# Two transformer layers on one core: the end of the first attention in another order

## The chip, the core and the metric

One core of a Trainium2 chip runs the whole program. Its engines are TensorE (PE, with its weight loads PEld), VectorE (DVE), ScalarE (ACT), GpSimd (POOL) and SyncE (SP), which only issues DMAs here. The metric is the device time of one launch in microseconds.

## The reference

Four residual steps on x of shape (2, 1024, 128), each on a layernorm of x. The change lies between the end of the first and the beginning of the routed part of the second.

```
x = x + attention0(layernorm(x))   # 8 heads, low-rank queries and keys, softmax over 1024 keys, W_O
x = x + ffn0(layernorm(x)):
      shared = (silu(h @ shared_gate.T) * (h @ shared_up.T)) @ shared_down.T       # width 352
      probs = softmax(h @ gate_w.T); the 2 best of 8 experts, weights normed
      routed = sum over the 2 experts of weight * the same ffn with the expert's weights
x = x + attention1(layernorm(x))   # 16 heads of 8, rope, causal
x = x + ffn1(layernorm(x))         # 2 of 8 experts for the whole sequence, gelu
```

## The kernel before

The 2048 tokens are 16 tiles of 128, 4 chunks of 512, 2 batches of 1024. There is no planner: each engine has its own list of instructions, in an order written out by hand, and the lists meet in semaphores (`wait_ge`, `then_inc`). An engine that waits holds up all that stands behind it in its list.

**The first attention** runs in 16 units (u = 0 to 15) of two heads. In a unit, k goes over 8 key tiles of 128. For each k there are four `scores` (i = 0 to 3: two heads by two query chunks), ACT's exponentials of them (`exp0`, L907), and `values` (L1353), which multiplies them by the compressed values. The denominators are sums of the exponentials over the keys: the tiles of a pair of k are added (`pair_adds` on POOL, `last_sums` on DVE in the last unit, L2079), and `denominators(u, pp, j)` (L1361) multiplies the sum of pair j by ones, for j = 0 to 3. `exp0` for an even k waits until the pair sum before it has read the same buffer. `denominators` of j = 0 waits for `rden_ok`, the four reciprocals (`context_rden`, L2070) of the unit before, which read the same PSUM bank; the unit's own last one (j = 3) is called in the next unit. In the table `DEN0_AT` stands at which k which j is called.

In the last unit PE has no scores for maxima to do, and other work lies beside it: the norm of batch 0 is turned (`second_turns`), `gate_logits(0, c)` are made at k = 2 and 3, DVE makes `probabilities(0)`, `probabilities_normed(0)`, `ranks(0)` and, after PE's `expert_counts(0)` (at k = 7), `slots(0)`, which gives the row that each token goes to.

**From the last unit to the routed blocks.** POOL's `scatter(0)` is 16 indirect DMAs (L641) that wait for `slot_ok`. SP's `load(0)` (L510) waits for all of them, and PE's `block_x_turns(0)` (L1597) for the load. ACT and DVE split the turned rows into a high and a low part (`block_x_hi`, `block_x_lo`), and `block_up(0)` (L1624 to L1626) is the first product of the routed experts. It also waits for the low parts of all eight experts' weights (`w_lo_ok`) and for the table of experts (`block_ok`). Four experts' weights are split early; for the `LATE_EXPERTS` ACT makes `hi_weights` and DVE `low_weights` (L2203).

Meanwhile the rest of the attention and the shared expert run: the last `denominators`, `last_context` (four reciprocals and two products, L2088), `o_mms(2)` and `o_mms(3)` (output products of batch 1, L1374), `add_output1` (L2096), `second_stats`, `half_var`, `quick_rstd` (the norm's factor), `norm_chunk(2)` and `norm_chunk(3)` (L1967), `second_turns(2)` and `(3)` (L1387), `gate_logits(1, ...)` (L1393). The shared expert goes by chunk c and third f of its width: `shared_up(c, f)` (L1540, gate and up), ACT's `shared_silu` (L1018), DVE's `shared_hidden(c, f)` (L2334), then `shared_down(c)` (L1554) and `shared_add(c)` (L2339). In the kernel before only chunks 0 and 1 are done here. `shared_up` number n = 3c + f waits for `h_done` n - 1, n = 1 for the context's bank and n = 3 for the bank of the denominators.

Of the kernel before, what the change touches and what calls it, by code (L numbers as in the profile page):

```python
# [46 lines left out]
NCH = T // CH  # L47
# [86 lines left out]
Z0_FIRST = 2  # L134
Z0_AT = {1: (1, 3), 3: (2, 0), 4: (2, 1)}
TURN0_AT = {(5, 1): 0, (6, 0): 1, (6, 1): 2, (7, 0): 3}
DEN0_AT = {3: 0, 5: 1, 7: 2}

# [84 lines left out]
def build(nc, d, out):  # L225
    with ExitStack() as ctx:
# [206 lines left out]
            g = HP * ((c + pp) % 2) + h  # L433
            return slice(DC * g, DC * (g + 1))
        XT_BANK, ROUTE_BANKS, XNT1_BANKS, OUT_BANKS = 7, (7, 6), (0, 1, 6, 7), (2, 2, 4, 5)
        DOWN_BANKS = (4, 5, 6, 3)
        FRONT_BANKS = (6, 6, TURN1_BANK, TURN1_BANK)

        OUT1_TURN_BANKS, OUT1_BANKS, LAST_BANKS = (0, 1, 4, 5), (0, 1, 6, 7), (0, 1, 4, 5)
# [417 lines left out]
        def _(act):  # L857
# [152 lines left out]
            def shared_silu(c, fs=range(3)):  # L1010
                for f in fs:
                    n, m = 3 * c + f, FM[f]
                    act.wait_ge(eg_mm, n + 1)
                    if n == 0:
                        act.wait_ge(pair_add, U0 * NPAIR * HQ)
                    if n >= 2:
                        act.wait_ge(h_done, n - 1)
                    nc.scalar.activation(silu_pt(n)[0:m], ps[0:m, gate_bank(n), :], ACT.Silu).then_inc(silu_done, 1)  # L1018

            shared_silu(0, range(2))  # L1020
            for e in LATE_EXPERTS:
                hi_weights(e)
            shared_silu(0, range(2, 3))
            shared_silu(1)
            second_xnT(2)
            second_xnT(3)
# [223 lines left out]
        def _(pe):  # L1250
# [126 lines left out]
            def second_turns(c):  # L1377
                pe.wait_ge(ln_xn, NT + (c + 1) * TC)
                if c == 0:
                    pe.wait_ge(max_done, U0 * NMX0)  # L1380
                if c == 2:
                    pe.wait_ge(ctx_T, U0)
                    pe.wait_ge(h_done, 2)
                if c == 3:
                    pe.wait_ge(slot_ok, 1)
                for t in range(TC):
                    ins = nc.tensor.transpose(ps[:, XNT1_BANKS[c], t * P:(t + 1) * P], xn[:, c * TC + t, :], ident[:])  # L1387
                ins.then_inc(ln_turn, 1)
# [22 lines left out]
            def unit0(u, pp):  # L1411
# [10 lines left out]
                for k in range(TS):  # L1422
# [10 lines left out]
                        values(u - 1, 1 - pp, TS - 1)  # L1433
                    if k == 1 and u:
                        denominators(u - 1, 1 - pp, NPAIR - 1)
                    if k in DEN0_AT:
                        denominators(u, pp, DEN0_AT[k])
                    turn(k, 0)
                    for i in range(2, HQ):
                        scores(u, pp, k, i)  # L1440
# [101 lines left out]

            def shared_down(c, ts=range(TC)):
                pe.wait_ge(h_done, 3 * c + 3)
                if c < 2:
                    pe.wait_ge(o_add, 3 + c)
                elif c == 2:
                    pe.wait_ge(slot_ok, B)
                else:
                    pe.wait_ge(h_done, 3 * c + 2)  # L1550
                for t in ts:
                    for f in range(3):
                        m = FM[f]
                        ins = mm(ps[:, DOWN_BANKS[c], t * P:(t + 1) * P], hidden_pt(3 * c + f)[0:m, t * P:(t + 1) * P],  # L1554
                                 wm[0:m, E0, 2 * F0 + f * D:2 * F0 + (f + 1) * D], start=(f == 0), stop=(f == 2))
                if TC - 1 in ts:
                    ins.then_inc(ed_mm, 1)

            pe.wait_ge(wm_in, 16)
            denominators(U0 - 1, 1, NPAIR - 1)  # L1560
            shared_up(0, range(2))
            for c in range(2, NCH):
                o_mms(c)
            shared_up(0, range(2, 3))
            shared_up(1)
            shared_down(0)
            second_turns(2)
            second_turns(3)
            shared_down(1)
            gate_logits(1, 0)  # L1570
# [391 lines left out]
        def _(dve):  # L1962
# [118 lines left out]
            def last_context(u):  # L2081
                for q in range(4):
                    context_rden(u, q)
                dve.wait_ge(rden_ok, 4 * (u + 1))
                dve.wait_ge(ctx_T, u + 1)
                for c in range(QH):
                    rows = half_rows(u, c)
                    v.tensor_tensor(ctxT[rows, u // UH, u % UH // 2, c, :], cT[rows, 1, :], cT[rows, 0, :],  # L2088
                                    ALU.mult).then_inc(ctx_out, 1)
# [256 lines left out]
            ranks(0, 1)  # L2346
            slots(0)
            last_sums(3)
            block_experts(0)
            last_context(U0 - 1)  # L2350
            shared_hidden(0, 0)
            shared_hidden(0, 1)
            for n, e in enumerate(LATE_EXPERTS):
                dve.wait_ge(w_hi_ok, n + 1)
                low_weights(e)
            for c in range(2, NCH):
                add_output1(c)
                second_stats(c * TC, (c + 1) * TC)
                shared_hidden(0 if c == 2 else 1, 2 if c == 2 else 0)
            half_var(1, 1)  # L2360
            quick_estimate(1)
            shared_hidden(1, 1)
            quick_newton(1)
            shared_hidden(1, 2)
            quick_newton(1)
            quick_newton(1)
            dve.wait_ge(half_step, hs.n)
            norm_chunk(2)
            norm_chunk(3)
            shared_add(0)  # L2370
            shared_add(1)
            probabilities(1)

# [379 lines left out]
```

## Time and profile before

| what | value |
|---|---|
| median of 3 runs | 847.03 us (844.85, 847.03, 851.38) |
| profiled execution | 852.06 us, its span 850.2 us |
| mean granted clock of TensorE | 0.974 of full |
| PE busy | 778.2 us, 92% |
| DVE, ACT, POOL busy | 613.6, 505.9, 411.1 us |

Times in all rows are microseconds from the span's start of the one profiled execution. A value in brackets at the end of a row is how long the engine was idle before it, and the instruction that ended this idle time. The granted clock is in parts of full speed: 1.00 is 2.4 GHz and 0.50 is 1.2 GHz.

### The profile page before, as it was taken

The page shows a single profiled execution, that of the slowest core. Times are in us where ns is not written, and L with a number is a line of the kernel's source. Part 1 is how long each engine was busy: PE and PEld are TensorE (multiplying, and loading weights), DVE is VectorE, ACT ScalarE, POOL GpSimd, SP SyncE. Part 2 cuts the span into 40 slices and gives each one's busy share as a digit, 9 for nine tenths or more (in the row PEclk, how much of TensorE's full clock was granted, in tenths as well). Part 3 has the DMA queues.
Part 4 walks back from the last instruction along what each step waited for, and adds up shares of the span by engine and source line. Part 5 has one row for each costly group of instructions (what it writes and reads, how often), then busy time and mean ns, then how long its engine had stood idle before and what let it go on. Part 6 is the DMA issues. An engine that isn't in the chain of part 4 may idle for free.

```text
span 850.2 us, 13859 instructions
## 1 busy us (share of the span) xinstructions
PE 778.2 (92%) x4602; PEld 454.9 (54%) x4602; DVE 613.6 (72%) x1611; ACT 505.9 (59%) x864; POOL 411.1 (48%) x466
## 2 busy tenths in 40 slices
PE   5899999999999988889999988789999999999986
PEld 2354444444444433378978865445555455554554
DVE  5878687786877895966336669777778778788555
ACT  3336665757656574445646555467767777776672
POOL 3505866677666682634242577886353232220121
PEclk9979999999999996999999999899999999999999
DMA  9300000000000000022222112000000000000001
GB/s 348 147 18 1 1 1 1 1 1 1 1 1 1 2 1 1 31 85 82 66 81 70 35 37 83 22 10 1 1 2 1 1 2 1 1 1 1 2 1 50
DMA packets 14539, 25.35 MB, mean 30 GB/s; under 512 B 3174, under 2 KB 9192, under 8 KB 14344
## 3 DMA queue, kind: packets, MB, share of 16 engines
q1 hardware_dynamic: 11798, 18.85, 6.5%
q0 software_dynamic: 2048, 4.20, 1.7%
q10 hardware_dynamic: 626, 1.43, 0.5%
q8 instruction: 40, 0.66, 0.3%
q14 instruction: 27, 0.22, 0.1%
HBM read 15.03 MB, written 9.44 MB: 29 GB/s over the span
## 4 chain that ended last, share of the span: by engine, by line
PE 36%; DVE 15%; POOL 6%; issue 3%; ACT 1%; DMA 0%; ACTq 0%; POOLq 0%; DVEq 0%
PE ps L1671 6%; PE ps L1756 6%; PE ps L1736 4%; DVE ps L2529 3%; PE ps L1642 3%; DVE mx_part L2532 3%; PE ps L1624 2%; PE ps L1626 2%; PE ps L1625 2%; PE ps L1634 1%; POOL xnT L659 1%; PE ps L1540 1%; PE ps L1589 1%; PE ps L1764 1%; PE ps L1825 1%
## 5 line engine op out<-in xcount | busy, mean ns | idle before, releaser
L2047 DVE TENSOR_REDUCE mx_part<-ps 128x1 f32<-128x512 f32 x256 | 163.8, 682 | 58.5 <-PE ps L1320 57.8
L1112 ACT ACTIVATE pt<-ps 128x1024 f32<-128x1024 f32 (+1 forms) x160 | 149.7, 938 | 69.5 <-PE ps L1736 68.2
L907 ACT ACTIVATE pt<-ps 128x512 f32<-128x512 f32 x256 | 140.9, 596 | 76.8 <-PE ps L1345 70.0
L1671 PE MATMUL ps<-rounded 128*128 128x128 f32 (+2 forms) x352 | 124.3, 387 | 11.5 <-DVE mx_part L2529 3.8
L2529 DVE CUSTOM_DVE_ANT_0 ps<-ps,wm 128x128 f32<-128x128 f32 (+3 forms) x256 | 119.5, 518 | 18.3 <-PE ps L1671 17.1
L1345 PE MATMUL ps<-rounded 100*128 100x512 f32 x256 | 122.3, 491 | 10.3 <-ACT pt L907 9.5
L859 ACT ACTIVATE rounded<-ps 128x512 fp32r<-128x512 f32 (+3 forms) x160 | 94.4, 592 | 62.3 <-PE ps L1309 22.1
L722 POOL TENSOR_SCALAR_AFFINE_SELECT pt<-pt 128x512 f32<-128x512 f32 x64 | 39.9, 636 | 167.1 <-ACT pt L1112 167.0
L1736 PE MATMUL ps<-rounded 128*128 128x512 f32 (+2 forms) x352 | 115.5, 368 | 0.7 <-ACT rounded L859 0.7
L1320 PE MATMUL ps<-rounded 98*128 98x512 f32 x256 | 104.9, 427 | 2.6 <-DVE mx_part L2047 1.4
L2532 DVE TENSOR_REDUCE mx_part<-ps 128x1 f32<-128x512 f32 x128 | 82.4, 686 | 30.9 <-PE ps L1671 30.5
L1345 PEld LDWEIGHTS ps<-rounded 100*128 100x128 f32 x256 | 47.6, 192 | 83.2 <-ACT pt L907 46.7
L1671 PEld LDWEIGHTS ps<-rounded 128*128 128x128 f32 x352 | 64.1, 192 | 45.8 <-DVE mx_part L2532 19.5
L1756 PE MATMUL ps<-pt,wm 128*9 128x512 f32 (+3 forms) x768 | 77.8, 493 | 5.5 <-POOL pt L722 5.4
L1736 PEld LDWEIGHTS ps<-rounded 128*128 128x128 f32 x352 | 62.5, 188 | 37.4 <-issue 17.8
L588 POOL TENSOR_TENSOR xn<-pt 128x512 f32<-128x512 f32 x48 | 60.3, 1280 | 46.0 <-ACT pt L907 46.0
L588 POOL TENSOR_TENSOR xnT<-pt 128x512 f32<-128x512 f32 x48 | 60.4, 1279 | 33.3 <-ACT pt L907 33.3
L1353 PE MATMUL ps<-pt,ckv 128*32 128x512 f32 x512 | 69.9, 619 | 0.9 <-ACT pt L907 0.9
L1320 PEld LDWEIGHTS ps<-rounded 98*128 98x128 f32 x256 | 48.8, 193 | 25.8 <-issue 19.4
L641 POOL DMA_INDIRECT to_experts<-xn,slot_i x32 | 33.9, 1060 | 45.8 <-DVE slot_i L2297 36.6
L2469 DVE TENSOR_TENSOR pt<-ps,pt 128x352 f32<-128x352 f32 x46 | 24.1, 523 | 40.5 <-ACT pt L1059 39.8
L859 ACT ACTIVATE pt<-ps 128x128 f32<-128x128 f32 (+2 forms) x94 | 36.4, 388 | 22.4 <-PE ps L1634 13.6
(308 smaller groups left out, 1296.4 us busy)
## 6 DMA issues: line engine op xcount, KB each, us to landing
wm<-in_wm SPq DMA_DIRECT2D x1, 4896.0 KB, 15.8
to_experts<-kstage SPq DMA_DIRECT2D x6, 512.0 KB, 4.6
of_experts<-pt SPq DMA_DIRECT2D x12, 256.0 KB, 2.0
kstage<-to_experts SPq DMA_DIRECT2D x10, 256.0 KB, 2.8
wm<-in_experts SPq DMA_DIRECT2D x1, 1540.0 KB, 7.6
x<-in_x SPq DMA_DIRECT2D x4, 256.0 KB, 6.2
out<-x SPq DMA_DIRECT2D x4, 256.0 KB, 2.3
early<-in_wo ACTq DMA_DIRECT2D x1, 512.0 KB
```

The source lines that it names most:

```text
L588: nc.gpsimd.tensor_tensor(sums(u, j)[i], pt0(0, i), pt0(1, i), ALU.add).then_inc(pair_add, 1)
L859: return nc.scalar.activation(dst, src, ACT.Copy)
L907: nc.scalar.activation(pt0(k, i), ps[:, ST0_BANKS[i % 2], :], ACT.Exp, scale=SCALE0).then_inc(exp_done, 1)
L1112: nc.scalar.activation(pt[:, 4 * (t % 2) + 2 * g:4 * (t % 2) + 2 * g + 2, 0:w], ps[:, ST1_BANKS[2 * g]:ST1_BANKS[2 * g] + 2, 0:w], ACT.Exp ...
L1320: mm(ps[:, max_bank(u, n), :], cq[0:NZ, b * S + j * P:b * S + (j + 1) * P], key_stack[u % 2][0:NZ, h, c * CH:(c + 1) * CH], start=True, st ...
L1345: mm(ps[:, ST0_BANKS[i % 2], :], key_stack[pp][0:NZM, h, k * P:(k + 1) * P], query_stack[pp][0:NZM, h, c * CH:(c + 1) * CH], start=True, s ...
L1671: ins = mm(bank[:, o:o + w], queries1(u, i), keys[:, 0:w], start=(o == 0), stop=(o == parts[-1][1]))
L1736: ins = mm(ps[:, ST1_BANKS[r], o:o + w], keys[:, j % TC * P:(j % TC + 1) * P], queries1(u, (c + 1) * TC - w // P, w // P), start=(o == 0), ...
L1756: ins = mm(ps[RS * r:RS * r + DH + 1, CTX_BANK, CH - w:CH], v_cur[pp][:, j, r, :], pt[:, 4 * (t % 2) + r, o:o + w], start=(j == CTX1_START ...
L2047: v.tensor_reduce(mx_part[u % 2][:, o:o + 1], ps[:, max_bank(u, n), :], AX_X, ALU.max).then_inc(max_done, 1)
L2529: v.tensor_tensor_reduce(tile, tile, later[:, CH - w:CH], 1.0, NEG, ALU.add, ALU.max, dst).then_inc(max1_done, 1)
L2532: v.tensor_reduce(dst, tile, AX_X, ALU.max).then_inc(max1_done, 1)
```

## The change

It computes the same and has the same instructions. In the last unit `denominators` of pair 0 is called at k = 4 instead of k = 3. On PE `shared_up(0, 0)` goes ahead of the unit's last `denominators`, the other two thirds of chunk 0 ahead of `o_mms`, `shared_down(0)` ahead of `shared_up(1)`, and the last third of `shared_up(1)` between `second_turns(2)` and `second_turns(3)`. `shared_down(0)` writes bank 7 instead of 4 and waits for `slot_ok` instead of `o_add`; `second_turns(3)`, which writes bank 7 as well, waits for `shared_add(0)`. On DVE `shared_hidden(0, 0)` goes between the first and the second reciprocal, the other two of chunk 0 behind the context products, the norm's factor is computed in one piece, `shared_add(0)` goes ahead of the norm, and `low_weights` and `block_experts(0)` go behind it. On ACT the third silu goes between the second and the third `hi_weights`.

```diff
-DEN0_AT = {3: 0, 5: 1, 7: 2}
+DEN0_AT, DEN0_LAST_AT = {3: 0, 5: 1, 7: 2}, {4: 0, 5: 1, 7: 2}
...
-        DOWN_BANKS = (4, 5, 6, 3)
+        DOWN_BANKS = (7, 5, 6, 3)
...
             shared_silu(0, range(2))
-            for e in LATE_EXPERTS:
+            for e in LATE_EXPERTS[:2]:
                 hi_weights(e)
             shared_silu(0, range(2, 3))
+            for e in LATE_EXPERTS[2:]:
+                hi_weights(e)
             shared_silu(1)
...
                 if c == 3:
-                    pe.wait_ge(slot_ok, 1)
+                    pe.wait_ge(moe_add, 1)
...
-                    if k in DEN0_AT:
-                        denominators(u, pp, DEN0_AT[k])
+                    den_at = DEN0_AT if u + 1 < U0 else DEN0_LAST_AT
+                    if k in den_at:
+                        denominators(u, pp, den_at[k])
...
             def shared_down(c, ts=range(TC)):
                 pe.wait_ge(h_done, 3 * c + 3)
-                if c < 2:
-                    pe.wait_ge(o_add, 3 + c)
+                if c == 0:
+                    pe.wait_ge(slot_ok, 1)
+                elif c == 1:
+                    pe.wait_ge(o_add, 4)
...
             pe.wait_ge(wm_in, 16)
+            shared_up(0, [0])
             denominators(U0 - 1, 1, NPAIR - 1)
-            shared_up(0, range(2))
+            shared_up(0, range(1, 3))
             for c in range(2, NCH):
                 o_mms(c)
-            shared_up(0, range(2, 3))
-            shared_up(1)
             shared_down(0)
+            shared_up(1, range(2))
             second_turns(2)
+            shared_up(1, [2])
             second_turns(3)
             shared_down(1)
...
             def last_context(u):
                 for q in range(4):
                     context_rden(u, q)
+                    if q == 0:
+                        shared_hidden(0, 0)
...
             last_sums(3)
-            block_experts(0)
             last_context(U0 - 1)
-            shared_hidden(0, 0)
             shared_hidden(0, 1)
+            shared_hidden(0, 2)
+            for c in range(2, NCH):
+                add_output1(c)
+                second_stats(c * TC, (c + 1) * TC)
+            half_var(1, 1)
+            quick_rstd(1)
+            shared_add(0)
+            norm_chunk(2)
+            shared_hidden(1, 0)
+            norm_chunk(3)
+            shared_hidden(1, 1)
             for n, e in enumerate(LATE_EXPERTS):
                 dve.wait_ge(w_hi_ok, n + 1)
                 low_weights(e)
-            for c in range(2, NCH):
-                add_output1(c)
-                second_stats(c * TC, (c + 1) * TC)
-                shared_hidden(0 if c == 2 else 1, 2 if c == 2 else 0)
-            half_var(1, 1)
-            quick_estimate(1)
-            shared_hidden(1, 1)
-            quick_newton(1)
-            shared_hidden(1, 2)
-            quick_newton(1)
-            quick_newton(1)
-            dve.wait_ge(half_step, hs.n)
-            norm_chunk(2)
-            norm_chunk(3)
-            shared_add(0)
+                if n == 0:
+                    shared_hidden(1, 2)
+            block_experts(0)
             shared_add(1)
             probabilities(1)
```

## Rows read from the trace of the kernel before

**Rows 1.** The page: the granted clock in 40 slices of 21.3 us.
```profile
PEclk9979999999999996999999999899999999999999
```

**Rows 2.** Windows: busy time of each engine, granted clock (PEclk), DMA.
```profile
320.50:321.00 0.50, 0.00 (x0) 0.00 (x0) 0.50 (x1) 0.00 (x0) 0.50 (x1) 0.77 0.00 0
...
334.00:334.50 0.50, 0.50 (x8) 0.00 (x0) 0.50 (x2) 0.00 (x0) 0.00 (x0) 0.58 0.00 0
...
344.00:348.00 4.00, 2.35 (x17) 0.54 (x18) 3.76 (x9) 1.83 (x3) 2.61 (x3) 1.00 0.05 16
...
375.50:376.00 0.50, 0.50 (x3) 0.50 (x3) 0.23 (x2) 0.48 (x2) 0.00 (x0) 0.50 0.59 225
```

**Rows 3.** Timeline of PE in the last unit: start, duration, instruction, count.
```profile
319.15 1.06 PE L1353 MATMUL ps<-pt,ckv 128*32 128x512 f32 x8
321.33 1.94 PE L1361 MATMUL ps<-half,ones 128*32 128x512 f32 x8 [1.11 <-DVE cT L2070]
...
341.25 1.04 PE L1361 MATMUL ps<-half,ones 128*32 128x512 f32 x8
```

**Rows 4.** Timeline of ACT in the last unit.
```profile
324.03 1.08 ACT L907 ACTIVATE pt<-ps 128x512 f32<-128x512 f32 x2 [3.89 <-PE ps L1345]
...
335.30 2.27 ACT L907 ACTIVATE pt<-ps 128x512 f32<-128x512 f32 x4 [3.12 <-PE ps L1345]
```

**Rows 5.** Timeline of DVE in the last unit.
```profile
317.90 3.38 DVE L2070 RECIPROCAL cT<-ps 128x128 f32<-128x128 f32 x4
...
324.66 1.29 DVE L2079 TENSOR_TENSOR early<-pt 128x512 f32<-128x512 f32 x2 [2.24 <-ACT pt L907]
...
330.87 0.22 DVE L2226 TENSOR_REDUCE g<-g 128x8 f32<-128x64 f32 x1 [4.36 <-ACT g L935]
...
333.67 1.29 DVE L2079 TENSOR_TENSOR half<-pt 128x512 f32<-128x512 f32 x2
...
340.48 0.22 DVE L2267 TENSOR_TENSOR big<-ps,kcount 128x64 f32<-128x64 f32 x1 [1.71 <-PE ps L1407]
...
343.98 2.50 DVE L2079 TENSOR_TENSOR early<-pt 128x512 f32<-128x512 f32 x4
```

**Rows 6.** Timeline of PE from the last unit to the first block.
```profile
346.62 1.06 PE L1361 MATMUL ps<-early,ones 128*32 128x512 f32 x8 [1.66 <-DVE early L2079]
347.62 3.70 PE L1540 MATMUL ps<-xnT,wm 128*128 128x512 f32 x8
351.92 3.84 PE L1374 MATMUL ps<-vo,big 128*128 128x128 f32 x32 [0.60 <-DVE big L2088]
...
368.48 2.84 PE L1554 MATMUL ps<-wm,pt 128*128 128x128 f32 x24
...
372.86 0.64 PE L1597 MATMUL ps<-ident,kstage 128*128 128x128 f32 x4
375.01 0.42 PE L1624 MATMUL ps<-rounded 128*128 x1 [1.51 <-DVE x_lo L2463]
```

**Rows 7.** Timeline of DVE after the last unit.
```profile
353.70 3.28 DVE L2203 TENSOR_TENSOR rounded<-wm,rounded 128x704 fp32r<-128x704 f32 x4
356.90 0.68 DVE L2096 TENSOR_TENSOR x<-ps,x 128x512 f32<-128x512 f32 x1
...
363.81 0.69 DVE L2334 TENSOR_TENSOR pt<-ps,pt 96x512 f32<-96x512 f32 x1 [0.43 <-PE ps L1540]
...
365.66 2.27 DVE L1967 TENSOR_SCALAR xn<-x,mv,lnv 128x128 f32<-128x128 f32 x8
```

**Rows 8.** Timeline of POOL: the eighth and the last of sixteen scatters.
```profile
354.26 3.55 POOL L641 DMA_INDIRECT to_experts<-xn,slot_i  x1 [0.30 <-issue]
...
366.95 0.95 POOL L641 DMA_INDIRECT to_experts<-xn,slot_i  x1 [0.30 <-issue]
```

**Rows 9.** SyncE's DMA queue: two first loads; landing of the first five.
```profile
369.19 0.80 SPq L510 DMA_DIRECT2D kstage<-to_experts  x2
...
DMA to landing us min/median/max: 2.7/3.0/3.7
```

## The prediction

> **What bounds the kernel now.** I read the page first: TensorE (PE) is busy 92% of the span (the table above), and the row of granted clock has one dent inside the first attention's end, at the slice that begins near 319 us [rows 1]. Then the windows: the clock falls between 320.5 and 321 us from 2.4 to 1.2 GHz and comes back at 334.1, while a stretch with more idle PE, 344 to 348, keeps it [rows 2]. Then the timelines of PE, ScalarE (ACT) and VectorE (DVE) over the last unit, and of PE, DVE, GpSimd (POOL) and SyncE's queue from there to the first routed block. The reader should see two stages. Up to 344 us a loop over the three engines is in charge, not PE's load: the exponentials of key tile k+1 need the pair sums of DVE, these need the exponentials of tile k, these PE's scores. From 344 to 375 us a chain that alternates between PE and DVE is in charge, with POOL's sixteen scatters as a second chain close beside it. From 375 us on PE is nearly full, so what is won before it should reach the end whole: nothing later is tied to an absolute time.
>
> **Part 1, denominators(15, 0) from k = 3 to k = 4.** In front of PE's scores (3,2) and (3,3) stands denominators of pair 0, which waits for the reciprocals of unit 14. DVE makes these from 317.90 to 321.28; PE stands 1.11 us and starts at 321.33, by then at 1.2 GHz [rows 3, 5]. Behind it come the scores, their exponentials at 324.03 after 3.89 us of idle ACT, their sums at 324.66 after 2.24 us of idle DVE [rows 3 to 5].
> After the change scores (3,2) follow values(2) at about 320.1 (319.15 and 1.06 us [rows 3]; their bank is free by then). Their exponentials (2.27 us for four, 0.57 each) lie under the reciprocals. DVE goes on without a gap: four sums at 0.62 us from 321.2 end at 323.7 and probabilities(0), which needs gate_logits(0,1) at 321.3, at 324.2. The eight gate logits are 0.8 us (sixteen fit in between 371.3 and 372.86 [rows 6]). PE at 2.4 GHz does scores (4,0) and (4,1), values(3) (1.0) and denominators(0) (1.0, as the row at 341.25) from 321.3 and reaches scores (4,2) at 323.6; exponentials (4,2) and (4,3) end at 325.1, the gate's at 325.35. So probabilities_normed starts at 325.4, where it was 330.87: 5.5 us earlier. From there the steps of before: 2.8 us to last_sums(2) (330.87 to 333.67), four sums 2.5 (ends 330.7), the rest of the ranks about 1.5 (before, DVE's last piece ended at 338.77, that is 340.48 less the wait of 1.71), expert_counts about 0.5 (an estimate below that wait of 1.71), so slots(0) begins at 332.7 instead of 340.48, **7.8 us** earlier; before, the exponentials (5,2) to (6,1) only came at 335.30 because denominators(1) and values(4) ran at half clock [rows 3 to 5]. The last exponential is done at 336.0 and slots at 336.2, so last_sums(3) (343.98 before) moves by the same 7.8.
> How much of this is order and how much clock? The same hand schedule for the old order at 2.4 GHz throughout: denominators(0) 321.33 to 322.25, exponentials (3,2) and (3,3) to 323.7, sums to 324.4, exponentials of tile 4 to 326.5, normed at 326.8, slots at 334.1. So the order is worth **1.4 us** and the clock's fall **6.4 us**. The fall is one event of one execution.
>
> **Part 2, from last_sums(3) to the first block.** I keep the times of before (last_sums(3) at 343.98) and take off the shift at the end. One third of shared_up is four matmul instructions, 1.72 us (3.44 between first and last start of eight, plus the tail). shared_up(0,0) fits in PE's wait of 1.66 us ahead of the last denominators, which stay at 346.62 [rows 6]. DVE then has nothing in 346.4 to 347.7 (block_experts, 1.3 us, stood there for free and now costs DVE 1.3 us later). Reciprocal 0 (0.85, a quarter of 3.38 [rows 5]) to 348.6, shared_hidden(0,0) 0.6 (like the one at 363.81 [rows 7]), three reciprocals and the context product: first half at 352.5, 0.6 us later than before. PE does shared_up(0,1) and (0,2) to 351.1 and waits 1.3 us; output products 352.5 to 356.05 (3.56 between starts, against 351.92), shared_down(0) 2.7 us to 358.75, no longer behind add_output1; shared_up(1,0..1) to 362.2.
> DVE: two hidden products to 354.3, first add and statistics to 356.2, second add at 356.35. From 356.90 to 365.66 before are 8.8 us, of which four hidden products (0.6 each) and the wait of 0.43 fall away and 1.8 are the first chunk: 4.1 us, so the norm is known at 360.5 [rows 7]. shared_add(0) to 361.2; norm_chunk(2) to 362.35, hidden(1,0) to 362.95, norm_chunk(3) to 364.1, hidden(1,1) to 364.7, first low part (0.82 us of the 3.28) to 365.5, hidden(1,2) to 366.15. PE: turns of chunk 2 at 362.4, shared_up(1,2) 363.0 to 364.8, turns of chunk 3, wait of 0.8 for hidden(1,2), shared_down(1) 366.2 to 368.9 (368.48 to 371.16 before), gate logits 1.7 us: block_x_turns(0) could start at **370.6** instead of 372.86. Three low parts and block_experts end at 369.9, ahead of block_up(0), which costs nothing while its cover, the 2.15 us from block_x_turns(0) to block_up(0), stays. The moved wait of second_turns(3) for moe_add 1 (shared_add(0), 361.2) is over before norm_chunk(3); the split of the high weights on ACT lies in ACT's idle time.
> The other chain is POOL's. Its last scatter ends at 367.9, the load is issued at 369.19 and took 2.7 to 3.7 us (its line in rows 9), so the rows were there between 371.9 and 372.86: without a faster scatter the gain is at most 1.0 us. One scatter took 3.55 us, the others 0.96 [rows 8, 9]. It began at 354.26, inside DVE's four low parts (353.70 to 356.98) and ended 0.83 after them. I take it that these products with both inputs in SBUF hold up POOL. The change puts the low parts at the end of the scatters: 2.6 us less, and perhaps 1.0 again on the sixteenth. Load landed between 369.3 and 371.3. Value taken: 371.0, a gain of **2.0 us** (bounds 0 and 2.3).
> The Trainium skill, "SBUF — State Buffer", section "Who interferes with whom", infers that a tensor_tensor leaves descriptor generation alone; by that, the long scatter has another cause and stays, and this term is at most 1.0 instead of 2.0. The row speaks against the page, as a coincidence in time only.
>
> **The sum.** Against the profiled execution (852.06 us, span 850.2): 7.8 + 2.0 = 9.8, hence 842.3. Against the median of 847.03: the three runs lie at 844.85, 847.03 and 851.38, and 852.06 less the fall's 6.4 is 845.7, so I read the lower two as runs without it and the upper one as one with it. Then the median loses 1.4 + 2.0 = 3.4: 843.6. Between the two, I predict **843.0**.
>
> **Rivals.**
> (a) The fall is in most executions of before and the change always removes it: 847.03 - 9.8 = 837.2. For it: the profiled run and one of three show it, and the change removes just the wait in which it fell. Against: the middle run lies nearer to the lowest than to the highest. 0.16.
> (b) The clock falls at another wait, slower than before. The price is the 6.4 us just worked out, the place PE's new wait of 1.3 us ahead of the output products or the one at expert_counts (about 0.7, after scores with gaps); 843.0 + 6.4 = 849.4. It decides if the fall comes in more than half of the executions. For it: 1.11 us of idle was enough at 320.2, and 1.51 ahead of 375.01, where the clock is down at 375.5. Against: 1.66 us at 345 was not, and PE's waits from 344 to 375 add up to about 3.8 us instead of 5.3 [rows 2, 6]. 0.18.
> The Trainium skill, "TensorE: Matmul & The Clock Gate", section "A second HAM failure mode: psum-queue depth-cycling", says that frequent short idles between groups of matmuls make the clock oscillate; by that rule this rival would be the outcome, and the trace agrees in one of the two waits that are longer than 1.5 us.
> (c) The scatter stays long, or the late low parts and block_experts hold up the first block: part 2 gives 0 to 1.0, so 844.0 to 845.0. 0.18.
> (d) My forecast, 840 to 845: 0.48.
>
> **Range and chances.** Clear of no change by this kernel's measurement is about 1%, 8.5 us. The range takes in (c), (d) and half of each of (a) and (b): 837.5 to 848.5. Faster by over 1% (under 838.6) is (a), 0.16, and 0.01 for the dip at 375 gone as well: 0.17. Slower by over 1% (over 855.5) would need two falls: 0.04. The rest, 0.79, is within 1%.
>
> **What would show it.** Right: no PE wait for cT ahead of L1361 near 321; ACT's idle of 3.89 us and DVE's of 4.36 much shorter; slots at least 1.4 us earlier; no scatter over 3 us in the middle of the sixteen; time from last_sums(3) to block_up(0) 29.0 us where it was 31.0; the granted clock full from 316 to 370. Wrong: PEclk at 0.50 anywhere from 322 to 370, DVE's second add later than 12.4 us after last_sums(3), SyncE's first load still 25.4 us after slot_i, or PE waiting for L2203 or L2311 ahead of L1624.

## The result and the profile after

The changed kernel takes 841.66 us (median of 20 runs, 838.84 to 847.80) where the kernel before, run beside it, takes 847.24 (20 runs, 842.09 to 854.46): ratio 0.9946, 95% interval 0.9926 to 0.9966. That is 5.6 us or 0.5% faster, inside the 1% that I had named as this kernel's bound, and 1.3 us from the 843.0 predicted. Here and below a ratio leaves disturbed runs out on both sides, so it can differ a little from the quotient of the medians beside it. On another chip, as the experiments show, the same kernel is 1.1% slower than the one before.

The profiled execution took 842.36 us, its span is 840.5 where it was 850.2. The page's row of the clock has no dent near 319 us any more (compare [rows 1]):

```profile
PEclk9879999999999999999999999999999999999999
```

The windows of the changed kernel confirm it; columns as in [rows 2]. From 316 to the first block the granted clock is 1.00, and it stays so when the block begins, where it was 0.50 before:

```profile
316.00:364.50 48.50, 42.33 (x258) 22.68 (x257) 40.94 (x108) 22.60 (x40) 24.03 (x21) 1.00 0.14 46
364.50:366.00 1.50, 1.48 (x8) 1.23 (x9) 0.65 (x3) 1.47 (x3) 0.00 (x0) 1.00 0.66 175
```

The timeline of PE, beside [rows 3] and [rows 6]:

```profile
321.25 1.04 PE L1363 MATMUL ps<-half,ones 128*32 128x512 f32 x8
...
336.32 1.98 PE L1543 MATMUL ps<-xnT,wm 128*128 128x512 f32 x4
338.24 1.06 PE L1363 MATMUL ps<-early,ones 128*32 128x512 f32 x8
...
344.13 3.84 PE L1376 MATMUL ps<-vo,big 128*128 128x128 f32 x32 [1.20 <-DVE big L2096]
...
357.88 2.94 PE L1559 MATMUL ps<-wm,pt 128*128 128x128 f32 x24 [0.62 <-DVE pt L2342]
360.67 1.85 PE L1395 MATMUL ps<-gw,xnT 128*128 128x8 f32 x16
362.37 0.63 PE L1603 MATMUL ps<-ident,kstage 128*128 128x128 f32 x4
364.52 0.42 PE L1630 MATMUL ps<-rounded 128*128 x1 [1.51 <-DVE x_lo L2468]
```

The reader should see that the denominators at 321.25 have no wait in brackets (1.11 us before), that shared_up(0, 0) at 336.32 fills the wait that stood ahead of the last denominators, and that block_x_turns(0) at 362.37 follows the gate logits with no wait: its rows had landed, PE's own order sets its start. DVE, beside [rows 5] and [rows 7]:

```profile
316.02 3.38 DVE L2076 RECIPROCAL cT<-ps 128x128 f32<-128x128 f32 x4
319.32 2.42 DVE L2085 TENSOR_TENSOR early<-pt 128x512 f32<-128x512 f32 x4
...
324.02 0.22 DVE L2234 TENSOR_REDUCE g<-g 128x8 f32<-128x64 f32 x1 [1.89 <-ACT g L935]
...
331.90 0.23 DVE L2275 TENSOR_TENSOR big<-ps,kcount 128x64 f32<-128x64 f32 x1 [1.02 <-PE ps L1409]
...
335.40 2.50 DVE L2085 TENSOR_TENSOR early<-pt 128x512 f32<-128x512 f32 x4
...
348.02 0.68 DVE L2104 TENSOR_TENSOR x<-ps,x 128x512 f32<-128x512 f32 x1
...
356.35 0.88 DVE L2211 TENSOR_TENSOR rounded<-wm,rounded 128x704 fp32r<-128x704 f32 x1
...
357.75 2.48 DVE L2211 TENSOR_TENSOR rounded<-wm,rounded 128x704 fp32r<-128x704 f32 x3
```

POOL and SyncE's queue, beside [rows 8] and [rows 9]. No scatter is longer than the first one, and the load is issued 2.3 us after the last begins:

```profile
336.21 1.59 POOL L641 DMA_INDIRECT to_experts<-xn,slot_i  x1 [11.66 <-DVE slot_i L2305]
...
356.20 0.95 POOL L641 DMA_INDIRECT to_experts<-xn,slot_i  x1 [0.30 <-issue]
```
```profile
358.45 0.80 SPq L510 DMA_DIRECT2D kstage<-to_experts  x2
```

**Where the 9.7 us between the two profiles lie.** I use two stages in all that follows. Stage 1 runs from the first of unit 14's four reciprocals to last_sums(3); stage 2 from there to block_up(0). Stage 1 was 317.90 to 343.98, 26.08 us, and is 316.02 to 335.40, 19.38. Stage 2 was 31.03 and is 29.12. So 6.70 and 1.91 us are the change's; another 1.88 had arisen before it (317.90 against 316.02), where nothing was changed, and 0.79 was given back behind block_up(0) (475.19 against 475.98 us to the end of the span). The sum is 9.70.

### The profile page after: what moved, and what is told of

It reads as the page before. It is cut to its first block, busy times and chain, and to the rows that moved or that the text cites. A ratio compares the mean times of both kernels' runs of the same rounds, so it can differ in the third digit from the quotient of the medians.

```text
span 840.5 us, 13859 instructions
## 1 busy us (share of the span) xinstructions
PE 770.1 (92%) x4602; PEld 451.0 (54%) x4602; DVE 613.3 (73%) x1611; ACT 505.5 (60%) x864; POOL 408.9 (49%) x466
## 4 chain that ended last, share of the span: by engine, by line
PE 36%; DVE 14%; POOL 6%; issue 4%; ACT 2%; DMA 0%; ACTq 0%; POOLq 0%; DVEq 0%
PE ps L1677 6%; PE ps L1762 6%; PE ps L1742 4%; DVE ps L2534 3%; PE ps L1648 3%; DVE mx_part L2537 3%; PE ps L1630 2%; PE ps L1640 2%; PE ps L1631 2%; PE ps L1632 2%; POOL xnT L659 1%; PE ps L1595 1%; PE ps L1770 1%; PE ps L1831 1%; PE ps L1543 1%
## 5 line engine op out<-in xcount | busy, mean ns | idle before, releaser
L1355 PE MATMUL ps<-pt,ckv 128*32 128x512 f32 x512 | 68.2, 605 | 0.9 <-ACT pt L907 0.9
L641 POOL DMA_INDIRECT to_experts<-xn,slot_i x32 | 31.8, 992 | 41.5 <-DVE slot_i L2305 32.4
L859 ACT ACTIVATE pt<-ps 128x128 f32<-128x128 f32 (+2 forms) x94 | 36.3, 388 | 22.6 <-PE ps L1640 13.8
```

The source lines that it names most:

```text
L859: return nc.scalar.activation(dst, src, ACT.Copy)
```

## The experiments

Theory: stage 1 gains 1.4 us by order and the rest by the clock; stage 2 gains since DVE's low parts no longer hold up a scatter. Rivals: the clock falls anyway at another wait; the long scatter has another cause. Four kernels ran on each of three chips, called S, T and U, with the kernel before beside them. A stage is read from the one profiled execution of each kernel. Its median was 878.47 on S, 877.34 on T and 846.52 on U.

| kernel | chip | median us | ratio to before (95%) | stage 1 | stage 2 | longest scatter after the first |
|---|---|---|---|---|---|---|
| a_den_only | S | 876.65 | 0.9963 (0.9928 to 0.9997) | 19.38 | 31.05 | 3.56 |
| b_rest_only | S | 889.97 | 1.0143 (1.0082 to 1.0204) | 20.70 | 41.5 | 1.18 |
| c_low_early | S | 878.81 | 1.0003 (0.9972 to 1.0033) | 19.39 | 33.21 | 4.10 |
| d_low_late | S | 889.67 | 1.0118 (1.0068 to 1.0168) | 20.70 | 43.2 | 0.96 |
| after_again | T | 888.07 | 1.0108 (1.0049 to 1.0167) | 19.40 | 41.5 | 1.19 |
| e_den_low | T | 887.79 | 1.0106 (1.0053 to 1.0159) | 19.39 | 43.2 | 0.96 |
| f_fill | T | 878.51 | 1.0008 (0.9981 to 1.0036) | 20.68 | 31.08 | 3.56 |
| g_turn_early | T | 888.36 | 1.0119 (1.0070 to 1.0168) | 19.39 | 41.65 | 1.21 |
| before_again | U | 846.40, one run | | 20.70 | 31.08 | 3.55 |
| h_one_pause | U | 843.96 | 0.9988 (0.9958 to 1.0017) | 19.38 | 31.75 | 2.70 |
| i_three_pauses | U | 844.27 | 0.9997 (0.9971 to 1.0024) | 19.38 | 32.35 | 2.69 |
| j_early_three | U | 844.71 | 0.9980 (0.9951 to 1.0010) | 19.39 | 33.09 | 2.70 |

**a_den_only**, the kernel before with the new place of the denominators alone.
```diff
-DEN0_AT = {3: 0, 5: 1, 7: 2}
+DEN0_AT, DEN0_LAST_AT = {3: 0, 5: 1, 7: 2}, {4: 0, 5: 1, 7: 2}
...
-                    if k in DEN0_AT:
-                        denominators(u, pp, DEN0_AT[k])
+                    den_at = DEN0_AT if u + 1 < U0 else DEN0_LAST_AT
+                    if k in den_at:
+                        denominators(u, pp, den_at[k])
```


> The kernel before with one edit: in the last unit denominators of pair 0 is called at k = 4. Stage 1 is the time from the first reciprocal of unit 14 to last_sums(3) (26.1 us before, 19.4 after the change), stage 2 from last_sums(3) to block_up(0) (31.0 before, 29.1 after). Order theory: stage 1 is 19.4 us if the clock stays at 2.4 GHz, stage 2 stays at 31.0; median 1.4 us under before, and up to 3 us if falls of the clock near the reciprocals become rarer. Rival, clock only: the order itself gives nothing, stage 1 of a run of the old order without a fall is also 19.4, and the median differs from before by less than 1 us unless the falls vanish.

**b_rest_only**, the changed kernel without it.
```diff
-DEN0_AT, DEN0_LAST_AT = {3: 0, 5: 1, 7: 2}, {4: 0, 5: 1, 7: 2}
+DEN0_AT, DEN0_LAST_AT = {3: 0, 5: 1, 7: 2}, {3: 0, 5: 1, 7: 2}
```


> The changed kernel with denominators of pair 0 back at k = 3. Stage 2 is 29.1 us as in the changed kernel, the sixteen scatters have none over 1.6 us. Stage 1: with a fall of the clock 26 us, without one 20.8 (order theory) or 19.4 (clock only). Median: before less 1.9 us.

Stage 1 is 19.38 against 20.70 us: with the clock full in both, the order alone is worth 1.3. In a the rest is as before, long scatter and stage 2 of 31.05 included, and its median gains 1.8 us. But b is 1.4% slower, which no theory of mine had: stage 2 takes 41.5 us. Its chain of waits, in order of time, names what:

```profile
349.45 0.28 DVE mv L2112 x4
349.73 9.48 another core or an unknown queue
359.21 0.02 issue
359.24 0.70 DVE x L2104
```

Only one core runs, so the 9.48 us between the first chunk's statistics and the second chunk's addition are a wait that the profile can't name.

**c_low_early**, the changed kernel with the low parts ahead of the two output additions, so that they lie in the middle of the scatters again.
```diff
             shared_hidden(0, 2)
+            for n, e in enumerate(LATE_EXPERTS):
+                dve.wait_ge(w_hi_ok, n + 1)
+                low_weights(e)
             for c in range(2, NCH):
...
             shared_hidden(1, 1)
-            for n, e in enumerate(LATE_EXPERTS):
-                dve.wait_ge(w_hi_ok, n + 1)
-                low_weights(e)
-                if n == 0:
-                    shared_hidden(1, 2)
+            shared_hidden(1, 2)
```


> The changed kernel with the four low parts of the weights back ahead of the output additions. Port theory: one scatter that begins beside them takes about 3.5 us, as before; the norm is known 3.3 us later and block_x_turns(0) comes 2.5 to 3.3 us later than in the changed kernel, stage 2 about 32. Rival (what the Trainium skill, SBUF - State Buffer, section Who interferes with whom, infers for tensor_tensor): all scatters stay near 0.96 us, and the long one of before had another cause; stage 2 is then the same 32, as PE and DVE set it.

**d_low_late**, the kernel before with nothing but the same loop moved the other way, behind norm_chunk(3).
```diff
-            for n, e in enumerate(LATE_EXPERTS):
-                dve.wait_ge(w_hi_ok, n + 1)
-                low_weights(e)
             for c in range(2, NCH):
...
             norm_chunk(3)
+            for n, e in enumerate(LATE_EXPERTS):
+                dve.wait_ge(w_hi_ok, n + 1)
+                low_weights(e)
             shared_add(0)
```


> The kernel before with one edit: the four low parts go behind norm_chunk(3). Port theory: no scatter over 1.6 us in the middle, the first load is issued about 2.6 us earlier counted from slot_i (25.4 before). The chain of DVE loses 3.3 us ahead of the norm, PE's own work then sets the end: stage 2 about 29.3, nearly all of what the whole change wins in stage 2. Rival, the orders on PE and of the denominators carry it: stage 2 stays within 0.7 us of 31.0.

The long scatter follows the low parts. Timelines of DVE and POOL of c_low_early:

```profile
343.27 3.28 DVE L2211 TENSOR_TENSOR rounded<-wm,rounded 128x704 fp32r<-128x704 f32 x4
```
```profile
341.78 1.21 POOL L641 DMA_INDIRECT to_experts<-xn,slot_i  x1 [0.30 <-issue]
343.29 4.10 POOL L641 DMA_INDIRECT to_experts<-xn,slot_i  x1 [0.30 <-issue]
347.69 0.95 POOL L641 DMA_INDIRECT to_experts<-xn,slot_i  x1 [0.31 <-issue]
```

The scatter ends at 347.39, 0.84 us after the last low part (346.55). Before, the same two ends were 357.81 and 356.98, 0.83 apart; in a_den_only and f_fill they are 0.84 apart. In d_low_late all fifteen later ones take 0.96 or less. So the cause is the low parts, and the price is set by where they end. The 1.21 us in the changed kernel fits too: that scatter began at 344.42, beside the last context product (64x512, both inputs in SBUF), which ended at 344.79, and ended 0.84 us after it. But not every such instruction holds a scatter to its end: the four sums of `last_sums(3)` (128x512, inputs in SBUF, 335.40 to 337.90) lie beside the first scatter, which took 1.59 us, and it was done at 337.80, before the last sum.

c also divides what stage 2 gained. It does not stall in batch 0, and its stage 2 of 33.21 us, where I had expected about 32, stands against 29.12 in the changed kernel: in the new order the place of the low parts is worth 4.1 us. The rest of the new order without it is 2.2 us worse than the old one (33.21 against 31.05 in a_den_only). Together they make the 1.9 us. This compares profiles of different chips; where nothing stalls, the old order's stage 2 is the same on all of them (31.03, 31.05, 31.08 and 31.08).

The stall came back in d, with 43.2 us in stage 2, and not in c. So it is not part of the new order of PE or of the denominators: moving the low parts behind the scatters is enough to bring it.

**after_again** is the changed kernel itself, **e_den_low** the kernel before with the edits of a and d together.

> The changed kernel itself, as the measure for the other three on the same chip. Stage 1 (first reciprocal of unit 14 to last_sums(3)) 19.4 us, stage 2 (last_sums(3) to block_up(0)) 29.1, the ratio to before 0.995.

> The kernel before with two edits: denominators of pair 0 at k = 4, the four low parts behind norm_chunk(3). Nothing else of the change. If the place of the low parts carries stage 2: stage 1 19.4, stage 2 29.3 (PE's own work sets it), all scatters under 1.6 us, median within 1 us of the changed kernel. Rival, the new orders on PE and of the denominators carry it: stage 2 above 30.3 and the median 1.5 to 2 us above the changed kernel.

Both stall and are 1.1% slower than the kernel before on chip T. The windows of after_again, over the scatters of batch 0 and then of batch 1:

```profile
346.00:356.00 10.00, 4.54 (x28) 3.78 (x28) 1.84 (x9) 0.00 (x0) 7.83 (x9) 0.86 0.14 49
392.00:400.00 8.00, 4.62 (x32) 3.91 (x30) 5.94 (x24) 2.32 (x5) 6.13 (x7) 1.00 0.30 109
400.00:412.00 12.00, 3.66 (x15) 3.39 (x15) 0.53 (x1) 1.23 (x3) 9.25 (x10) 0.68 0.16 54
```

The columns are PE, PE's loads, DVE, ACT, POOL, the clock, the DMA share, GB/s. While POOL goes on at its pace of one in 1.27 us, PE is busy for a third to a half of the time and DVE and ACT hardly at all. The waits that the trace names no cause for ("remote" or "issue") give the times. The timelines of DVE and ACT:

```profile
357.88 0.69 DVE L2104 TENSOR_TENSOR x<-ps,x 128x512 f32<-128x512 f32 x1 [9.51 <-remote]
```
```profile
400.67 0.28 ACT L859 ACTIVATE pt<-ps 128x128 f32<-128x128 f32 x1 [4.58 <-remote]
```
```profile
407.18 0.53 DVE L2474 TENSOR_TENSOR pt<-ps,pt 128x352 f32<-128x352 f32 x1 [8.66 <-remote]
```

The row of batch 0 lasts from 334.56 to 355.37, and DVE stands from 348.37, 13.8 us after it began. The row of batch 1 lasts from 392.04 to 412.03; ACT stands from 396.09, 4.1 us after it began, and DVE from 398.52. So the stall doesn't begin at a fixed place in the row. It ends with the row: by 3 us after it all three engines run again.

The kernel before on chip U, in the corresponding stretches of its batch 1, has DVE, ACT and PE at work (scatters from 381.67 to 401.67):

```profile
381.00:389.00 8.00, 7.71 (x55) 6.90 (x55) 7.00 (x29) 4.76 (x11) 5.80 (x6) 1.00 0.33 107
389.00:401.00 12.00, 11.80 (x92) 11.51 (x91) 3.99 (x8) 7.50 (x18) 8.95 (x11) 1.00 0.38 118
```

And a_den_only, on chip S, has the stall in batch 1's scatters and in the gathers, where nothing interrupts the row, but not in batch 0's, where the eighth scatter took 3.56 us:

```profile
346.00:356.00 10.00, 9.42 (x39) 5.00 (x39) 9.82 (x33) 2.71 (x6) 8.26 (x6) 1.00 0.13 42
383.00:391.00 8.00, 5.00 (x35) 4.27 (x33) 6.29 (x26) 2.48 (x6) 5.81 (x6) 1.00 0.35 107
391.00:403.00 12.00, 3.91 (x15) 3.47 (x15) 0.53 (x1) 0.74 (x2) 9.20 (x10) 0.54 0.17 56
```

This divides the eight kernels on S and T without exception: a, c and f, whose scatter of batch 0 is interrupted in the middle by the low parts, don't stall there; b, d, e, g and the changed kernel do. Whether it is the interruption that keeps the stall away, or only that the low parts lie inside the row and not behind it, these kernels can't tell, since in them the two always go together. The kernel before is some 30 us slower on these chips than on U. Its other rows of indirect DMAs, which nothing interrupts, would account for much of it if they stall as a's do (DVE's waits with no cause named are 12.07 us in batch 1's scatters, 7.17 and 6.55 us in the gathers), but it was not profiled there.

**f_fill**, the kernel before with one product that nobody reads ahead of the wait for the reciprocals, to fill part of it.
```diff
+                    if u == U0 - 1 and k == 3:
+                        pe.wait_ge(wm_in, 16)
+                        mm(ps[:, 0, :], wm[:, E0, 0:P], wm[:, 0, 0:CH], start=True, stop=True)
                     if k in DEN0_AT:
```


> The kernel before with one matmul of 128x512 on data that nobody reads (two instructions, 0.86 us) put into PE's wait of 1.11 us ahead of denominators of pair 0. Its order is the old one. If the clock falls because PE stands there, the falls near that place vanish and the median drops by their share times 5.4 us (0.5 to 2.5 us), with a higher mean granted clock than before, and stage 1 is 20.7 us. Rival, the fall has nothing to do with that wait: mean granted clock and median as before, within 1 us.

Stage 1 is 20.68 us and the ratio 1.0008, so the fill gains nothing that can be measured on T: at most 1.7 us by the interval's end. If the clock fell at this wait in most executions there, the median should have moved by most of 5.4.

**g_turn_early**, the changed kernel with block_x_turns(0) in the middle of shared_down(1) and the gate logits ahead of both, the DVE and ACT orders to match.
```diff
-            shared_down(1)
             gate_logits(1, 0)
             gate_logits(1, 1)
+            shared_down(1, range(0, 2))
...
             block_x_turns(0)
+            shared_down(1, range(2, TC))
```


> The changed kernel with a new end of stage 2: gate_logits(1) ahead of shared_down(1), so that the exponentials of the gate and both table loads of ACT lie under PE's work; block_x_turns(0) between the two halves of shared_down(1), so that the split of the rows lies under the second half. Expected: block_up(0) 1.2 us earlier (stage 2 27.9) and the first block's silu about 2 us earlier, so 2.0 us under the changed kernel. Rival: the load of the rows lands too late for the earlier turns, or the wait moves to DVE's low parts, and the median stays within 0.7 us of the changed kernel.

The wait ahead of block_up(0) fell from 1.51 to 0.17 us, but the stall of batch 0's scatters (stage 2 of 41.65) hid what that is worth. It was tried again in j.

The last four were meant for a chip that stalls; the one they ran on, U, behaves like that of the first profiles. **before_again** is the kernel before. **h_one_pause** is the changed kernel with an existing memset of 1.8 us on POOL moved into the middle of scatter(0); **i_three_pauses** has such a memset in scatter(0), in scatter(1) and between the two gathers; **j_early_three** is i with g's order.
```diff
+            def pause(n):
+                if n:
+                    pool.wait_ge(first_zero, n)
+                nc.gpsimd.memset(first_stack[:, 0:HG, :].bitcast(F32), 0.0).then_inc(first_zero, 1)
...
                 for k in range(TOPK):
+                    if k:
+                        pause(b)
                     for i in range(TS):
...
             scatter(0)
-            nc.gpsimd.memset(first_stack[:, 0:HG, :].bitcast(F32), 0.0).then_inc(first_zero, 1)
             scatter(1)
...
             gather(0)
+            pause(2)
             gather(1)
...
-                    dve.wait_ge(first_zero, 1)
+                    dve.wait_ge(first_zero, 3)
```


> The kernel before, unchanged, to have its own trace from the chip on which the other kernels of this study ran and took some 30 us more than on the first one. If the long stalls belong to uninterrupted trains of sixteen indirect DMAs on this chip: PE and DVE stand in the second half of scatter(1) and of the gathers, but not in scatter(0), whose 8th DMA is stretched to about 3.55 us by the low parts; span about 875 us. If they belong to something that the change brought: no stall of more than 3 us in the trains here, and the 30 us lie spread over the whole kernel. It also says whether the clock falls at the wait for the first four reciprocals here as in the first profile (then first reciprocal to last_sums(3) is about 26 us, otherwise 20.7).

> The changed kernel, with GpSimd's memset of first_stack (1.8 us, which stood behind scatter(0)) put between the 8th and the 9th indirect DMA of scatter(0). Theory (on this chip a train that runs on past some eight indirect DMAs makes the other engines stand, and the 2.6 us for which the low parts held up the 8th one in the kernel before kept that away): the stall of some 11 us in scatter(0) goes, last_sums(3) to block_up(0) is 30 to 32 us where the changed kernel had 41.5 here, and the time is about 877 where it was 888. Rival (low parts placed behind the train are the cause, by themselves, and no pause helps; or the number of DMAs in all counts): block_up(0) stays at 41 us or more from last_sums(3) and the time at 888.

> The changed kernel, with the same memset of 1.8 us three times: in the middle of scatter(0), in the middle of scatter(1), and between gather(0) and gather(1); the reader of first_stack waits for the third. Theory (pauses break the trains): no stall of more than 3 us on PE or DVE in any train, about 11 us less in scatter(0) and together some 25 us less in scatter(1) and the gathers, so some 850 us on this chip, 3% below the kernel before. Rival (only scatter(0) gains, since the stalls of scatter(1) and the gathers have another cause): 877. Rival (no pause helps): 888 to 892.

> The kernel of three pauses, with the block's turns of x ahead of the last three of unit 1's shared products, and its low parts ahead of the second shared addition (the order of g_turn_early). In g_turn_early PE waited only 0.17 us ahead of the first routed product where the changed kernel waits 1.51, but the stall of scatter(0) hid what that is worth. If that wait bounds: 1 to 2 us below the kernel of three pauses, about 849. If what PE gains there is lost behind (the scatter's landing bounds the first block, not the order of PE's work): the same as it within 0.5 us. If pauses do nothing: 888.

Whether a pause keeps the stall away could not be read, as chip U doesn't stall in any of them. What U did show are three other things.

First, the clock. before_again has the very wait in which it fell in the first profile, 1.11 us ahead of the same instruction, and it did not fall. The timeline of PE and the window around it:

```profile
318.01 1.06 PE L1361 MATMUL ps<-half,ones 128*32 128x512 f32 x8 [1.11 <-DVE cT L2070]
```
```profile
317.00:331.00 14.00, 11.63 (x64) 4.52 (x64) 10.36 (x21) 7.82 (x16) 3.38 (x3) 1.00 0.00 1
```

Stage 1 is 20.70, as in b and d, which have the wait too (1.11 and 1.12) and kept the clock. So the fall costs 26.08 - 20.70 = 5.4 us and came in one of four profiles with this wait. But the clock falls somewhere in many executions. Of the 25 runs of the kernel before on U that the ratios count, 12 had a mean granted clock of 0.980 or more (median 843.6 us) and 13 less (847.4). Of the changed kernel's 20 runs 19 had 0.980 or more and one 0.979. Where it falls in those runs is not in their records, and 0.980 only sorts them: the profiled executions of h, i and j have 0.982, 0.983 and 0.981 and a fall each, as the third point shows.

Second, the pause costs stage 2 something where there is no stall. The timelines of DVE and POOL of h_one_pause:

```profile
358.23 0.88 DVE L2212 TENSOR_TENSOR rounded<-wm,rounded 128x704 fp32r<-128x704 f32 x1
...
359.63 2.48 DVE L2212 TENSOR_TENSOR rounded<-wm,rounded 128x704 fp32r<-128x704 f32 x3
```
```profile
358.46 1.48 POOL L643 DMA_INDIRECT to_experts<-xn,slot_i  x1 [0.30 <-issue]
360.24 2.70 POOL L643 DMA_INDIRECT to_experts<-xn,slot_i  x1 [0.30 <-issue]
```

The pause of 1.8 us pushed the last two scatters into the late low parts. Again each ends 0.83 us after the low part beside it (359.94 and 359.11; 362.94 and 362.11), and PE waits 2.46 us for the load ahead of block_x_turns(0). In the changed kernel the sixteenth scatter began 0.15 us ahead of the first low part and took 0.95: it escaped by a hair. h's stage 2 is 31.75 against 29.12.

Third, g's order. j is 844.71 and i 844.27: no gain. Turns now precede half of shared_down(1), but PE waits 2.42 us for the load ahead of them: in i and j POOL's chain is in charge. The clock fell in all three kernels with a pause: in i in the wait of 2.59 us at this place, in h just behind its wait of 2.46 (1.00 from 366 to 367, 0.87 from 367 to 368, then 0.50), and in j before the wait, at 356, while PE was busy. The windows of i, then of j:

```profile
362.00:363.00 1.00, 0.00 (x0) 0.00 (x0) 0.00 (x0) 0.00 (x0) 0.00 (x0) 1.00 0.87 223
363.00:364.00 1.00, 0.25 (x1) 0.25 (x2) 0.00 (x0) 0.00 (x0) 0.00 (x0) 0.57 1.01 379
```
```profile
356.00:360.00 4.00, 3.33 (x17) 3.03 (x16) 2.09 (x8) 0.26 (x1) 1.65 (x1) 0.52 0.12 20
360.00:364.00 4.00, 2.25 (x11) 2.25 (x12) 0.47 (x1) 1.08 (x2) 0.00 (x0) 0.50 0.87 270
```

By its ratio to the kernel before, no version did better than the changed kernel (0.9946) on a chip of the first kind, nor than a_den_only (0.9963) on one of the second. The changed kernel itself did not run on U, nor a_den_only on T, so this compares ratios of different chips.

## Why the prediction was right, point by point

**The sum.** 843.0 was forecast and 841.66 measured, with the ratio's interval (0.9926 to 0.9966) giving 841.0 to 844.4 from 847.24. Against the profiled execution I had 842.3; it was 842.36, but that agreement is luck: 1.88 us of it came from ahead of the change, which I had not counted, and the two terms were 7.8 + 2.0 = 9.8 where 6.70 + 1.91 = 8.6 were measured.

**Part 1, order, 1.4 us.** Measured 1.31 (20.68 to 20.70 in four profiles with full clock, 19.38 to 19.40 in nine). Right.

**Part 1, the clock, 6.4 us.** Measured 5.4. This term was mis-sized: my hand schedules were about 1 us short of the truth at either order. By them stage 1 would have been 19.7 and 18.3 us, and it is 20.70 and 19.38. The rows of after say where: probabilities_normed begins 8.0 us after the first reciprocal (316.02 to 324.02) where I had 7.5, and slots(0) 7.9 after that where I had 7.3, since DVE waits 1.02 us for expert_counts, which stands behind two more scores on PE; I had 0.5 for that, marked as an estimate.

**How often it falls.** "The fall is one event of one execution" was right for this wait, but I then read the lower two of the three runs of before as runs without a fall. On U about half of the runs of before have a low mean clock, wherever in the kernel it fell. Order (1.3 + 1.9 = 3.2) leaves 2.4 of the measured 5.6 us, and fewer runs with a low clock (1 of 20, against 13 of 25 on U, at 847.4 - 843.6 = 3.8 us each) would make about 1.8 of it. This is argued from mean clocks, not shown; the fill of the one wait gained nothing on T, and h, i and j, with the same stage 1, had 11 of 34 runs under 0.980, where the longer wait for the load is one more place for a fall. So the mechanism of both parts held in the profiles, but that the median came out 1.3 us from the forecast is in part luck: 843.0 was a value between two sums, one with 6.4 us for the clock and one with nothing, and what the clock gives back in the median was not worked out.

**Part 2, 2.0 us.** Measured 1.91, and 1.96 against before_again; it is the balance of 4.1 us won by the place of the low parts and 2.2 lost by the rest of the new order, which the sum did not separate. Step by step: the second addition 12.4 us after last_sums(3), measured 12.62; block_x_turns(0) at 27.0 (371.0), measured 26.97; the wait ahead of the output products 1.3, measured 1.20; the one ahead of shared_down(1) 0.8, measured 0.62. I had the load's landing as the last to come; in fact PE's order was, and PE reached the turns at the time that I had given for the load.

**The low parts and the scatter.** Right, and no longer a coincidence in time. With low parts beside it a scatter lasts until just after them, in eight profiles; beside other work no scatter after the first exceeds 1.21 us. The Trainium skill, "SBUF — State Buffer", section "Who interferes with whom", infers that a tensor_tensor leaves descriptor generation alone; the runs contradict it (0.96 us grows to between 3.55 and 4.10), at least for these products of 704 elements with both inputs in SBUF.

**The rivals.** (a), the fall always removed: 837.2 lies outside the interval. (b), the clock falls at another wait: not in the profile of after, but h and i show it, with waits of 2.46 and 2.59 us that are longer than any PE has there in after, and so it exists. The Trainium skill, "TensorE: Matmul & The Clock Gate", section "A second HAM failure mode: psum-queue depth-cycling", gives short idles as a cause; here the same idle of 1.11 us was followed by a fall in one profile of four. (c), the scatter stays long or DVE is late: no on the first chips. (d) happened.

**What I had no case for.** Slower by over 1% had 0.04, with two falls of the clock as its only way. On T the changed kernel is 1.1% slower, and on S its part without the new denominators is 1.4% slower, by a mechanism that no profile of the first chip shows. The step that would have had to name it is "2.6 us less" on POOL: I took an interruption of POOL's row of DMAs for pure loss, and on those chips it came with 10 to 12 us less in stage 2.

**What stays open.** Why PE, DVE and ACT stand during such a row, what distinguishes the chips (each was used in one session only, so a passing state of the chip isn't ruled out), and whether any pause of POOL would do instead of the low parts. The pause was tried, but not on a chip that stalls.

## What to carry to other kernels

A long row of indirect DMAs on GpSimd is a resource of its own: look at what DVE does beside it. Large products from SBUF can hold an indirect DMA until they end, and where nothing stalls it pays to place them outside the row (4.1 us of stage 2 between c_low_early and the changed kernel). On S and T the same move brought the stall and made stage 2 10 to 12 us longer than in a_den_only, so measure both places. Run a change of under 1% on more than one chip before you believe its sign; look in the chain for waits that nothing in the kernel explains. And take a dent of the clock in one profile as a draw: profile the kernel before a second time before you put its price into a sum.

## What the hardware did that I had not expected

Chips of two kinds, with the same program: 847 and 878 us for the kernel before. On the slower ones uninterrupted rows of sixteen indirect DMAs, at one in 1.27 us, leave DVE idle for 8.66 or 12.07 us with no named cause; on the faster ones the same rows at the same pace don't. Where the eighth DMA took 3.56 us instead of 0.96, the eight behind it ran without a stall. In the rows that do stall, an engine first stood after anything from 1.6 us (DVE in a's gathers, whose row begins at 444.49 and whose DVE stands from 446.04) to 13.8 us (DVE in batch 0 of after_again), so no single count of DMAs in the row sets it off.

A scatter that meets a low part ends 0.83 to 0.84 us after it in every one of the six cases read (before, a, c, f and twice in h); one that began 0.15 us ahead of a single low part was not held up at all, and the first scatter was not held to the end of the sums beside it.

ACT loads a table twice in the first block, 1.28 us each, around one exponential of the gate of 0.26 us, and the first silu of the block comes after the second; the kernel before did the same. The timeline of ACT in the changed kernel:

```profile
363.66 1.28 ACT L935 ACT_TABLE_LOAD   x1
364.95 0.26 ACT L935 ACTIVATE g<-g 128x64 f32<-128x64 f32 x1
365.23 1.28 ACT L1061 ACT_TABLE_LOAD   x1
366.52 0.82 ACT L1061 ACTIVATE pt<-ps 128x352 f32<-128x352 f32 x2
```
